# Two graph-attention layers: where the bias of the first values is added, and how the first head's row of targets is made

## What is computed

```python
# layer 1 (4 heads of 128), layer 2 (1 head of 256)
xl = (x @ W).reshape(B, N, H, F)
asrc = einsum('bnhf,hf->bnh', xl, a_src);  adst = einsum('bnhf,hf->bnh', xl, a_dst)
e = leaky_relu(asrc[:, :, None, :] + adst[:, None, :, :], 0.2)
attn = softmax(where(mask, e, -1e9), axis=1)            # over the sources
out = einsum('bsdh,bshf->bdhf', attn, xl) + bias        # elu after layer 1
x = layernorm(x + gat2(elu(gat1(x))))
# third: Wh = x @ W; e = leaky(s_i + s_j) where adj > 0; softmax over axis 1; leaky(att @ Wh)
x = layernorm(x + third(x))
```

## Time and profile before

| | |
|---|---|
| Median of 3 runs | 868.36 us (867.67 to 869.53) |
| The profiled execution | 867.59 us, of which the span of the profile is 865.8 us |
| Mean granted clock of TensorE | 0.989 |
| PE busy | 95% of the span |
| DVE busy | 87% |
| ACT busy | 81% |
| POOL busy | 34% |
| DMA | 82 GB/s on average |
| PE's share of the chain that ended last | 76% |

### The profile page before, as it was taken

One profiled execution on the slowest core, in us unless ns is written; L12 is line 12 of the kernel. 1 busy time (PEld: TensorE's weight loads), 2 busy tenths in 40 slices (PEclk: granted clock), 3 DMA queues, 4 the chain that ended last, 5 costly groups with the idle time before them and its releaser, 6 DMA issues.

```text
span 865.8 us, 16909 instructions
## 1 busy us (share of the span) xinstructions
PE 824.1 (95%) x5828; PEld 772.9 (89%) x5828; DVE 752.7 (87%) x1978; ACT 698.7 (81%) x1302; POOL 290.3 (34%) x245
## 2 busy tenths in 40 slices
PE   6798979999999999999999999999999999989896
PEld 4688879999999999999999999999999999888775
DVE  6867896989899898989989898998989899896766
ACT  2687858889797988979798897979888897978563
POOL 0002010135343523534351443435243353534422
PEclk9899989999999999999999999999999999999999
DMA  9221325141251525034142504315251421310002
GB/s 247 63 74 35 90 50 135 38 107 65 86 124 50 134 62 138 35 94 116 50 134 62 147 26 113 95 51 138 65 141 41 120 73 32 89 41 13 25 1 73
DMA packets 78819, 70.89 MB, mean 82 GB/s; under 512 B 39308, under 2 KB 57868, under 8 KB 78736
## 3 DMA queue, kind: packets, MB, share of 16 engines
q1 hardware_dynamic: 78736, 69.83, 30.3%
HBM read 52.83 MB, written 8.59 MB: 71 GB/s over the span
## 4 chain that ended last, share of the span: by engine, by line
PE 76%; DVE 11%; ACT 8%; issue 3%; DMA 1%; POOL 0%; SPq 0%; POOLq 0%; DVEq 0%; ACTq 0%
PE bUU L604 22%; PE bG L698 10%; PE bUU L626 10%; PE bUU L615 9%; PE bG L716 8%; PE bG L686 6%; DVE junk L1056 4%; PE bUU L594 2%; ACT att L835 2%; PE bA L564 2%; ACT att L850 2%; PE bB L564 1%; PE bG L677 1%; PE bG L713 1%; DVE att L1118 1%
## 5 line engine op out<-in xcount | busy, mean ns | idle before, releaser
L604 PE MATMUL bUU<-val,att 128*128 128x129 f32 x2048 | 249.6, 275 | 1.5 <-DVE att L1118 1.5
L604 PEld LDWEIGHTS bUU<-val,att 128*128 128x128 f32 x2048 | 240.2, 192 | 3.1 <-issue 2.1
L1118 DVE SCALAR_TENSOR_TENSOR att<-mask_n,att 128x2048 f32<-128x2048 bf16 x64 | 146.1, 2283 | 46.9 <-ACT att L850 46.0
L1056 DVE CUSTOM_DVE_ANT_0 junk<-mask_t,a_rows,val 128x512 bf16<-128x512 bf16 x168 | 124.0, 794 | 0.0
L850 ACT ACTIVATE att<-att 128x2048 f32<-128x2048 f32 x64 | 122.9, 1921 | 0.6
L615 PE MATMUL bUU<-val,att 128*128 128x257 f32 x480 | 113.1, 385 | 2.2 <-DVE att L1114 2.2
L626 PE MATMUL bUU<-val3s,att 128*128 128x256 f32 x480 | 108.3, 379 | 0.2 <-DVE res L1155 0.2
L1056 DVE CUSTOM_DVE_ANT_0 junk<-mask_t,bA,val 128x512 bf16<-128x512 bf16 x152 | 104.1, 740 | 3.9 <-PE bA L564 3.9
L615 PEld LDWEIGHTS bUU<-val,att 128*128 128x128 f32 x480 | 87.7, 190 | 18.2 <-ACT x L862 4.4
L626 PEld LDWEIGHTS bUU<-val3s,att 128*128 128x128 f32 x480 | 90.0, 190 | 12.3 <-DVE res L1155 0.6
L835 ACT ACTIVATE att<-bB,val 128x512 f32<-128x512 f32 x152 | 95.9, 722 | 5.2 <-PE bB L564 5.2
(11 more groups left out here) (134 smaller groups left out, 1818.0 us busy)
## 6 DMA issues: line engine op xcount, KB each, us to landing
adj_in<-in_adj_dram SPq DMA_DIRECT2D x16, 1024.0 KB, 5.7
a_rows<-a_rows_dram SPq DMA_DIRECT2D x56, 256.0 KB, 4.6
x_in<-in_x_dram SPq DMA_DIRECT2D x16, 512.0 KB, 4.8
a_rows<-b_rows_dram SPq DMA_DIRECT2D x28, 256.0 KB, 3.4
out_dram<-act SPq DMA_DIRECT2D x14, 512.0 KB, 2.8
b_rows<-b_rows_dram SPq DMA_DIRECT2D x14, 256.0 KB, 3.2
mask_t<-mask_n SPq DMA_TRANSPOSE x64, 4.2
a_rows_dram<-scores_t SPq DMA_DIRECT2D x56, 2.0 KB
```

The lines of the kernel that those rows point to most:

```text
L604: ins = nc.tensor.matmul(to[:, (d % 2) * FX:(d % 2 + 1) * FX], p[:, s, d * P:(d + 1) * P], val1[u.batch % 2][:, s, u.index // 2, values], ...
L1056: nc.vector.tensor_tensor_reduce(junk[:, b] if u.row else att[u.slot % 3][:, b], mask_t[u.batch % 4][:, b], a_rows[:, u.index] if u.by_dma ...
L1118: nc.vector.scalar_tensor_tensor(flat(p), mask_n[u.batch % 3][:, 0:NB * N], BIG, flat(p), ALU.add, ALU.min)\
```

## The change

1. `values_1` no longer multiplies ones by the bias: 128 matmuls (L713) fall away. `bias1` becomes a full tile, filled by four DMAs that spread the bias over all partitions, and GpSimd adds 1 to it once at the start. GpSimd then adds it to `val1`, one instruction of 128 x 516 for each block (`add_bias_1`), blocks 0 and 1 ahead of `set_diag`, blocks 2 and 3 ahead of `norm_2`. `attend_head` waits until all four blocks have it.
2. `targets_by_dma` now holds for head 0 too, from batch 2 on. PE's 4 transposes for it fall away in 14 batches, and DVE, SP and the DMA queues make one more row.
3. Each row of targets goes into the row of `a_rows` from which its own head's sources came, so a row of sources is fetched again only after that head's `leaky`. Source row 3 is fetched behind the next adjacency.
4. In slot 1 DVE makes head 2's row before `keep_edges` of head 0, not after it. On GpSimd `add_bias_2` goes ahead of `norm_scale` of the first norm.
5. At the start two DMAs of one bias row each and DVE's six small instructions (`shift_bias_1`) fall away.

```diff
-        self.targets_by_dma = self.by_dma and index >= 1
+        self.targets_by_dma = self.by_dma
...
-        b_rows = [a_rows[:, 0], a_rows[:, H - 1], sb("b_rows", [P, N])[:]]
...
-            def spread_scores(n):
+            def spread_scores(n, heads):
                 sp.wait_ge(a_stored, 16 * H * (n - 1))
-                for h in range(H):
+                for h in heads:
                     if n > 2:
-                        if h == H - 1:
-                            sp.wait_ge(leaky_done, (units[SLOTS * (n - 1) + 3].u + 1) * NB)
-                        elif h == 0:
-                            sp.wait_ge(leaky_done, (units[SLOTS * (n - 1) + 2].u + 1) * NB)
-                        else:
-                            sp.wait_ge(top_done, (units[SLOTS * (n - 1) + 1 + h].u + 1) * NB)
+                        sp.wait_ge(leaky_done, (units[SLOTS * (n - 1) + 1 + h].u + 1) * NB)
                     sp.dma_start(a_rows[:, h], a_dram[h].rearrange("(o n) -> o n", o=1).to_broadcast([P, N]))\
                         .then_inc(a_spread[h], 16)
-            def spread_targets(n, i):
-                sp.wait_ge(b_turned_ready, (H - 1) * (n - 2) + i + 1)
+            def spread_targets(n, h):
+                sp.wait_ge(b_turned_ready, H * (n - 2) + h + 1)
                 if n > 2:
-                    sp.wait_ge(b_spread[i], 16 * (n - 2))
-                sp.dma_start(b_dram[i].rearrange("(b q i) -> q b i", b=NB, i=32),
+                    sp.wait_ge(b_spread[h], 16 * (n - 2))
+                sp.dma_start(b_dram[h].rearrange("(b q i) -> q b i", b=NB, i=32),
                              b_turned[0:P:32 // NB, :]).then_inc(b_stored, 16)
-                sp.wait_ge(b_stored, 16 * ((H - 1) * (n - 2) + i + 1))
-                if i == 0:
-                    sp.wait_ge(top_done, (units[SLOTS * n + 1].u + 1) * NB)
-                elif i == 1:
+                sp.wait_ge(b_stored, 16 * (H * (n - 2) + h + 1))
+                if h == H - 1:
                     sp.wait_ge(arow_copied, n - 1)
-                elif n > 2:
-                    sp.wait_ge(leaky_done, (units[SLOTS * (n - 1) + 2 + i].u + 1) * NB)
-                sp.dma_start(b_rows[i], b_dram[i].rearrange("(o n) -> o n", o=1).to_broadcast([P, N]))\
-                    .then_inc(b_spread[i], 16)
+                else:
+                    sp.wait_ge(top_done, (units[SLOTS * n + 1 + h].u + 1) * NB)
+                sp.dma_start(a_rows[:, h], b_dram[h].rearrange("(o n) -> o n", o=1).to_broadcast([P, N]))\
+                    .then_inc(b_spread[h], 16)
...
+            for h in range(H):
+                c = h % 2 * FX
+                sp.dma_start(bias1[:, h // 2, c:c + F],
+                             b1.rearrange("(o n) -> o n", o=1)[:, h * F:(h + 1) * F].to_broadcast([P, F]))\
+                    .then_inc(b1_loaded, 16)
...
                 if n >= 2:
                     spread_targets(n, 0)
+                    spread_targets(n, 1)
                 if 4 <= n + 2 < B:
                     load_x(n + 2)
                 if n >= 2:
-                    spread_targets(n, 1)
+                    spread_targets(n, 2)
                 if 2 <= n + 1 < B:
                     store_scores(n + 1)
                 if n >= 2:
-                    spread_targets(n, 2)
+                    spread_targets(n, 3)
                 if 2 <= n + 1 < B:
-                    spread_scores(n + 1)
+                    spread_scores(n + 1, (0, 1, 2))
                 if n + 1 < B:
                     turn_mask(n + 1)
                 if 1 <= n + 2 < B:
                     load_adj(n + 2)
+                if 2 <= n + 1 < B:
+                    spread_scores(n + 1, (3,))
...
+            def shift_bias_1():
+                pool.wait_ge(b1_loaded, 16 * H)
+                for g in range(G):
+                    features = bias1[:, g].rearrange("p (c n) -> p c n", n=FX)[:, :, 0:F]
+                    nc.gpsimd.tensor_scalar(features, features, 1.0, 1.0, ALU.add, ALU.mult).then_inc(bias1_ready, 1)
+            def add_bias_1(n, blocks):
+                for b in blocks:
+                    pool.wait_ge(val1_ready, n * NB + b + 1)
+                    nc.gpsimd.tensor_tensor(val1[n % 2][:, b, :, 0:HC], val1[n % 2][:, b, :, 0:HC], bias1[:], ALU.add)\
+                        .then_inc(val1_biased, 1)
...
+            shift_bias_1()
+            pool.wait_ge(bias1_ready, G)
+            add_bias_1(0, range(NB))
...
-                if pos == 2 and 0 <= n - 2 < B:
-                    norm_scale(n - 2, 0, moments1, var1, rstd1)
                 if pos == 2 and 0 <= n - 1 < B:
                     if n >= 2:
-                        pool.wait_ge(b_turned_ready, (H - 1) * (n - 2) + 2)
+                        pool.wait_ge(b_turned_ready, H * (n - 2) + 3)
                     else:
                         pool.wait_ge(b_t_ready, units[SLOTS * n + 3].r + 1)
                     add_bias_2(n - 1)
                 if pos == 2 and 0 <= n - 2 < B:
+                    norm_scale(n - 2, 0, moments1, var1, rstd1)
                     pool.wait_ge(x1n_done, (n - 1) * NB)
                 if pos == 2 and 0 <= n - 3 < B:
                     residual_2(n - 3)
                 if pos == 4 and n + 1 < B:
                     if n >= 1:
+                        pool.wait_ge(zinv_ready, (units[g - 2].h + 1) * 2)
+                        add_bias_1(n + 1, (0, 1))
                         pool.wait_ge(b_t_ready, units[g + 1].r + 1)
                     set_diag(n + 1)
+                    if n == 0:
+                        add_bias_1(n + 1, (0, 1))
+                if pos == 4 and 0 <= n - 3:
+                    norm_scale(n - 3, 1, moments2, var2, rstd2)
+                if pos == 4 and n + 1 < B:
+                    if n >= 1:
+                        pool.wait_ge(y1_done, units[g - 2].h + 1)
+                    add_bias_1(n + 1, (2, 3))
                 if pos == 4 and 0 <= n - 3:
...
+                pe.wait_ge(val1_biased, (u.batch + 1) * NB)
...
-                    nc.tensor.matmul(to, ones_r[:], bias1[:, g], start=True, stop=False)
...
+                if pos == 1 and 2 <= n < B:
+                    tops(units[g + 2])
+                    shifted_targets(units[g + 2])
                 if this and this.row:
                     keep_edges(this)
                 if pos in (4, 5) and g < LAST - 1:
...
                 if older:
                     elu(older)
-                if pos == 1 and 2 <= n < B:
-                    tops(units[g + 2])
-                    shifted_targets(units[g + 2])
```

56 lines of the change are left out of this document (17 added, 39 removed).

## The result

| | before | after |
|---|---|---|
| Median | 868.68 us (867.67 to 869.53, 4 runs) | 878.09 us (876.54 to 881.71, 4 runs) |
| The profiled execution, its span | 867.59, 865.8 | 876.54, 874.8 |

The ratio is 1.0118, with a 95% interval of 1.0104 to 1.0132: the change costs 9.4 us. The forecast was +5.2 (873.5, range 866.5 to 885). The sign and the range held, the size did not: the loss is nearly twice as large, and the question of this part is where the other half comes from.

What follows compares the result with a forecast made beforehand. A loop through PE, DVE, DMA and ACT was taken as the bound, so PE's savings count nothing; 13 x (0.29 + 0.1 + 0.1) = 6.4, less 1.2 at the start, gives +5.2 us: 873.5 us, range 866.5 to 885.

Steps and rivals of the forecast that it cites:

- What bounds the kernel: A 50.00 us loop from L698 through PE, DVE, DMA and ACT back to L698; PE savings count nothing in batches 2 to 14.
- The term of the loop: Batches 2 to 14: each loop grows by 0.29 + 0.1 + 0.1 us, 6.4 us over 13 loops.
- the column: Head 0's column on DVE, between x_lo and head 1's column: 0.60 us for a DMA instead of 0.31, so +0.29.
- `norm_2` under head 0's maxima: GpSimd's last norm_2 instruction, started later, slows head 0's maxima on DVE: 0.1 us in the loop, bounds 0 and 0.5.
- two landings in time: ACT needs head 0's and head 1's rows, nearly level, and the later counts: 0.1 us, bounds 0 and 0.4.
- The start: Before the loops: earlier first DMA and eight fewer bias matmuls against four added DMAs: -1.2 us, bounds -2.5 and +1.
- The end: Batch 15 has no values to make and trades 0.29 for 0.43 us: no effect.
- The margin that I had worked out for the store: Output's store, waiting for norm_2, is issued 1.7 us ahead of head 0's column, so the delay is covered.
- rival D: norm_2 ends after 511.5 and its store holds up head 0's row: 1 us a batch, 886 us; chance 0.08.
- C: GpSimd's x_in starts ahead of head 0's keep_edges, which waits 2.4 us, some 2 in the loop: 894 us; chance 0.05.
- A: PE is the bound after all, so its 1.40 us a batch are gained: 849 us; chance 0.08.
- B: The loop gets no longer: landings 0.2 us shorter, GpSimd free, start gives 2.5: 868.4 us; chance 0.22.

Runs made afterwards that it cites:

- the loop cut: Kernel before, with ScalarE's copy of block 3 of the values moved ahead of head 1's exponential: 862.86 us, ratio 0.9941.
- the row alone: Kernel before with only points 2 to 4 (head 0's row by DMA, new order), bias still on PE: 868.48 us, ratio 0.9998.
- the bias alone: Kernel before with only points 1 and 5 (bias added by GpSimd), head 0's row still by PE: 872.89 us, ratio 1.0056.
- one half of the change: Kernel before with points 2 to 4 plus ScalarE's copy of block 3 ahead of head 1's exponential: 857.03 us, ratio 0.9869.

## Why the prediction was right in kind and half in size

**What bounds the kernel: right.** The 0.05 us between ACT's copy and the next L716 held in all eleven loops of after (0.05 to 0.06), and the kernel without bias matmuls lost and gained nothing in its loops. That "PE's own work and this loop are within some tenths" is now a number: with the loop cut PE's own work is 49.79 us, the loop was 49.96. Both readings of the earlier trace rows were nearly true, and only the order of the waits told which came first.

The Trainium skill (Perfetto Trace Analysis, "Identifying the Most-Contended Engine") would have one begin with the engine of the highest occupancy. Here that engine was PE, and 0.96 us a batch off it changed a loop by 0.00 us; the rule's advice paid (0.44 for 0.44) once the loop was cut.

**The term of the loop: right in its sum, not in its parts.** Forecast +0.49 a batch, measured +0.45. That the sum came so near is partly luck, since the parts missed both ways. The starts of L716 lie 49.63 to 50.77 apart in the eleven loops, not 50.3 to 50.8. From `x_lo` to head 1's turned column the forecast was 16.38 and the batch above shows 16.54:
- the column, forecast 0.29: the rows give 0.30, less the 0.14 of slack ahead of the reciprocal.
- `norm_2` under head 0's maxima, forecast 0.1: one maximum takes 0.95 us instead of 0.74, so 0.21.
- not foreseen: `norm_2` also runs under the third attention's little column, which takes 0.33 instead of 0.16.
- two landings in time, forecast 0.1: nothing. Head 0's row landed 4.94 us behind its column, not the 5.88 of head 1's, so ACT was through with head 0 and stood idle for 0.74 us when head 1's row came. DVE's path grew by 0.55 and the loop by 0.45: the way from column to copy was no longer than before.

The rows of after for the second and third, and for `norm_2` itself:

```profile
507.81 0.33 DVE L1101 SCALAR_TENSOR_TENSOR b_t<-top,low 128x4 f32<-128x4 f32 x1
...
512.34 0.95 DVE L1072 CUSTOM_DVE_ANT_0 junk<-mask_t,a_rows,val 128x512 bf16<-128x512 bf16 x1
...
506.33 7.09 POOL L465 TENSOR_SCALAR act<-res,moments,rstd 128x256 f32<-128x256 f32 x4
```

The additions themselves take 1.3 us each (forecast 1.2), and beside them `x_lo` takes 1.23 us, as without them. What GpSimd costs in the loop is `norm_2`, pushed later, as the prediction had it. The halves alone cost 0.21 and 0.18 a batch and together 0.45. DVE's path tells why, at least for the most part: over the eleven loops its mean is 16.00 us before, 16.13 with the row alone, 16.22 with the bias alone and 16.55 with both, and each half alone can use up the same 0.14 us of slack; 0.07 us are left over.

**The start: the sign was wrong.** The failed step is "Against it four DMAs of 64 KB stand ahead of the loads of x and the first mask's transposes. I take -1.2". Up to the start of batch 2's loop, where the forecast's loops begin, after is 2.6 us late, beyond the bound of +1. The loads, which I let weigh less than 0.5 us, cost 1.3 to 4.2 (above): DVE's first maxima wait for the mask, and PE and ACT for the maxima. The gain ahead of them was real: 1.2 us up to there without the bias matmuls (124.84).

That only +0.4 is left at batch 3 is luck. The loop of batch 2 took 52.10 us before, and 2.05 of its excess lies between L698 and `x_lo` (24.29 us, 22.24 in the loops behind it). The rows of TensorE's granted clock (1.00 is 2.4 GHz, 0.50 the lower level, 1.2) fit this: before, PE was busy for 1.36 of the 4 us from 120 on, the clock stood at 0.50 from 124 to 128 and at 0.67 from 128 to 132, and L698 started at 126.02, in the middle of it. In after PE was busy for 1.10 us of the same 4, the clock stood at 0.66 from 124 to 128 and at 1.00 from 128 on, and L716 started at 128.61, behind it. This is read from the traces and wasn't tried; the forecast has no term for it.

**The end: the step that failed most.** "The end (batch 15) has no values to make and trades 0.29 for 0.43: nothing" was off by 3.7 us. The same sentence holds the reason: with no values there is no `x_lo` on DVE, so head 0's column is turned 1.3 us earlier behind L716 (32.21 us, 33.50 in the batch shown), while `norm_2` takes 7.84 us instead of 7.09. The margin that I had worked out for the store, 1.7 us, is what the other batches show (`norm_2` ends at 513.42, the column comes at 515.15); in batch 15 it is -0.35. I had priced rival D with a condition for every batch and never put it to the one batch whose DVE work differs. C then followed from D: `keep_edges` came late enough to meet `x_in`.

Together: 9.0 us of span = 0.4 + 4.9 + 3.7. The forecast of -1.2 + 6.4 + 0 counts thirteen loops, of which the first (batch 2's) lies in the first stretch here and the last (batch 14's, which leads into batch 15 and has no `x_lo`) in the third; on the same stretches it is -0.7 + 5.4 + 0.5. So 1.1 of the missing 3.8 us are the start, 3.2 the end, and the loops took 0.5 less.

**Rivals.** A fell in both kernels that could show it. B held for neither half in its loops. That the row alone costs nothing in total comes from its start: before shows 52.10 us for the loop of batch 2 at a granted clock of 0.96, the row alone 50.01 at 1.00. There too the clock was lower earlier (0.64 from 120 to 124, ahead of its L698 at 126.60); that this is what the row alone gained was read from the traces and not tried. C and D were right as mechanisms, each for one batch.

## What to carry to other kernels

When two chains are within tenths of each other, cut the one that waits before you take work off the engine that looks full: 0.96 us a batch off PE were worth nothing in the loops, one swap of two instructions 5.7 us in all, and behind the swap one half of the change was worth 5.8 more. Test every margin in the odd batches, the first and the last: a margin of 1.7 us in eleven batches says nothing of a batch in which one engine has 1.2 us less to do. A queue that stores results should not stand ahead of a row that the path waits for.
